# The gap in front of the key stacks taken out of a cross-attention kernel

## The reference

```
x (256 x 512), ctx (25088 x 512)
# 1. cross attention with sigmoid scores, 16 heads of 32
q = layernorm(x) Wq^T / sqrt(32);  k = ctx Wk^T;  v = ctx Wv^T
x = x + (sigmoid(q k^T per head) v) Wo^T
# 2. causal self attention over the 256 rows without softmax, each row divided by exp(n)
# 3. feed-forward: silu(h w1) * (h w2), two gelu layers of 2048, and back to 512
```

## Time and profile before

| | kernel before |
|---|---|
| time, median of 3 | 1910.59 us (1910.14 to 1911.89) |
| profiled execution | 1911.86 us, span of its instructions 1910.1 us |
| TensorE: matmul busy, weight load busy | 1899.6 us, 1709.3 us |
| VectorE busy | 1199.5 us |
| ScalarE busy | 1016.6 us |
| matmuls L749, L774, L790, L810 | 4032, 4032, 3136, 6272 records |
| granted TensorE clock | full speed (2.4 GHz) in all 40 slices of the span |

### The profile page before, as it was taken

How to read it: one execution, slowest core, us unless ns; L and a number is a source line. 1 busy time by engine, 2 the same in 40 slices (tenths; PEclk the granted TensorE clock), 3 DMA queues, 4 the chain that set the end, 5 groups by cost and what they waited for, 6 DMA issues and landing times.

```text
span 1910.1 us, 50764 instructions
## 1 busy us (share of the span) xinstructions
PE 1899.6 (99%) x19347; PEld 1709.3 (89%) x19348; DVE 1199.5 (63%) x2109; ACT 1016.6 (53%) x1136; POOL 4.5 (0%) x17
## 2 busy tenths in 40 slices
PE   9999999999999999999999999999999999999999
PEld 8889999999898999999888999999988999867998
DVE  7576766667667576666766757666676675427322
ACT  5545455555545545555554555545455455544864
POOL 0000000000000000000000000000000000000000
PEclk9999999999999999999999999999999999999999
DMA  7556555555655645555565564555556555464784
GB/s 214 154 153 176 133 154 157 158 155 143 171 145 155 172 130 154 156 159 158 144 170 146 152 169 132 158 152 159 157 151 168 143 148 139 100 233 150 279 299 165
DMA packets 130730, 310.91 MB, mean 163 GB/s; under 512 B 33888, under 2 KB 36960, under 8 KB 112096
## 3 DMA queue, kind: packets, MB, share of 16 engines
q1 hardware_dynamic: 97696, 212.79, 41.9%
q10 hardware_dynamic: 32992, 97.53, 15.8%
HBM read 153.95 MB, written 0.52 MB: 81 GB/s over the span
## 4 chain that ended last, share of the span: by engine, by line
PE 98%; DVE 1%; ACT 0%; DMA 0%; issue 0%; DVEq 0%; ACTq 0%
PE kp L749 25%; PE vp L774 24%; PE sc L790 19%; PE acc L810 18%; PE ps L1572 6%; PE ps L1557 2%; PE py L1585 1%; PE qk_p L1281 1%; PE kp L836 1%; PE vp L853 0%; PE sc L870 0%; DVE w_lo L1208 0%; DVE ln_stats L72 0%; PE kp L1059 0%; PE vp L1050 0%; DMA probs<-wkT_dram 0%
## 5 line engine op out<-in xcount | busy, mean ns | idle before, releaser
L378 ACT ACTIVATE probs<-sc 128x1024 f32<-128x1024 f32 x784 | 769.7, 1025 | 730.4 <-PE sc L790 594.6
L749 PE MATMUL kp<-x_combos,weights_r 128*128 128x256 f32 x4032 | 536.0, 279 | 0.0
L749 PEld LDWEIGHTS kp<-x_combos,weights_r 128*128 128x128 f32 x4032 | 491.4, 188 | 28.7 <-issue 28.4
L774 PE MATMUL vp<-more_weights,x_combos 128*128 128x256 f32 x4032 | 515.6, 277 | 0.0
L774 PEld LDWEIGHTS vp<-more_weights,x_combos 128*128 128x128 f32 x4032 | 485.3, 188 | 0.6 <-issue 0.4
L790 PE MATMUL sc<-rows_r,k_stack_r 96*128 96x256 f32 x3136 | 436.4, 279 | 0.1
L790 PEld LDWEIGHTS sc<-rows_r,k_stack_r 96*128 96x128 f32 x3136 | 396.0, 188 | 2.8 <-issue 1.6
L591 DVE TENSOR_TENSOR parts<-parts,kp 128x512 f32<-128x512 f32 x240 | 164.5, 685 | 327.0 <-PE kp L749 327.0
L810 PE MATMUL acc<-probs,v 128*32 128x256 f32 x6272 | 354.4, 380 | 0.0
L810 PEld LDWEIGHTS acc<-probs,v 128*32 128x32 f32 x6272 | 195.9, 110 | 131.4
L528 DVE TENSOR_TENSOR x_combos<-ctx_raw,x_combos 128x512 fp32r<-128x512 f32 x240 | 166.2, 693 | 8.2
(11 more groups left out here) (164 smaller groups left out, 851.5 us busy)
## 6 DMA issues: line engine op xcount, KB each, us to landing
k_stack_r<-k_rows_hi SPq DMA_DIRECT2D x784, 64.0 KB, 2.3
k_stack_r<-k_rows_lo SPq DMA_DIRECT2D x784, 64.0 KB, 2.4
k_stack_r<-k_stack_r SPq DMA_DIRECT2D x196, 256.0 KB, 3.0
ctx_raw<-ctxT_dram ACTq DMA_DIRECT2D x48, 1024.0 KB, 6.3
weights<-w_all_dram ACTq DMA_DIRECT2D x176, 256.0 KB, 3.6
w_raw<-w_all_dram SPq DMA_DIRECT2D x44, 1024.0 KB, 4.8
weights<-wqk_dram SPq DMA_DIRECT2D x2, 1024.0 KB, 11.7
probs<-wvT_dram SPq DMA_DIRECT2D x2, 512.0 KB, 7.5
```

The source lines that it names most:

```text
L378: nc.scalar.activation(probs[:, place(par, n), :], sc[g % 2][:], ACT.Sigmoid).then_inc(probs_ready, 1)
L749: last = nc.tensor.matmul(k2[:, r, :], wk[i - 1][:, k, a, r * P:(r + 1) * P], xc[:, i - 1, k, b, :], start=i in FRESH and r == 0 and n == ...
L774: last = nc.tensor.matmul(v2[:, r, :], xc[:, i - 1, k, b, r * P:(r + 1) * P], wv_c[i - 1][:, k, a, :], start=i in FRESH and r == 0 and n == 0,
```

## The change

One line goes. The 192 bytes per partition in front of `k_stack` are no longer there, so `k_stack` begins 192 bytes lower, and so does every tensor that is allocated behind it in `cross_attention` (`parts`, `k_rows_hi`, `k_rows_lo`, `v`, `probs`, `ln_stats`, `ln_mv`). Counted as above, `k_stack`, `v` and `probs` move from 320 to 128, the place of `more_weights`. No instruction is added, removed or put elsewhere in the order. What is allocated for the self attention and the feed-forward part begins where it did.

```diff
@@ -132,7 +132,6 @@
         wk, wv_c = [first_w[:, i] for i in range(7)], [more_w[:, i] for i in range(7)]
         raw, tmp = sb("ctx_raw", [P, KE, CH]), sb("x_sum", [P, 2, HS])
 
-        gap("before_k_stack", 48)
         kst, kst_f32 = keep["two_types"](stack, "k_stack", [P, 2, 2, HG, 2, HS])
         parts_r, parts = keep["two_types"](stack, "parts", [P, 4, 2, HS])
         kc, vt = parts[:, 0:3], parts[:, 3]
```

## The result

The changed kernel takes 1947.2 us (median of 5 runs, 1945.3 to 1953.0) against 1910.3 us before (5 runs on the same chip): ratio 1.019, 95% interval 1.0176 to 1.0205. It is slower, as forecast, but by 37 us instead of 12. The direction held and the size did not: 1947 is the rival that I gave 0.30.

What follows compares the result with a forecast made beforehand. TensorE, busy 99%, was taken as the bound, by the distance of matmul starts. Scores gave +12 us, other main terms 0, the prologue -0.3 at most: 1910.6 + 12 = 1922.6, rounded 1923; range 1901 to 1952, the forecast's own 1914 to 1930.

Steps and rivals of the forecast that it cites:

- the rival that I gave 0.30: All key and value groups lose the fast rate, 1.41 us instead of 1.36: +30 us, total 1944 to 1953; chance 0.30.
- the first part: Whole kernel: TensorE busy 99%; time is the number of matmuls by the distance of their starts.
- the place of two operands modulo 512: Matmuls: moving less stationary place modulo 512 bytes sets the rate, 113.3, about 117.7 or 120 ns.
- (b): Scores: operand distance goes from 192 to 384, so they run at 120 ns, 0.96 us a group: +12 us.
- the 191 or 192 that I gave as a sign: Scores' weight loads: would last 191 or 192 ns in the mean instead of 188 if the forecast was right.
- the parity of 64-byte steps: Operand distances: odd multiples of 64 (64, 192) reach the floor; even ones (256, 384) collide and run at 120 ns.
- (c): Keys and values behind the scores: keep their distance of 64 and their places, so unchanged, 0.
- (d): Steps from values or keys to scores: at most 5 us lies there, not winnable with scores at 120 ns: 0.
- (e): `weigh`: `v` and `probs` move together, their distance stays 0: 0 us, bounds 6 us either way.
- (f): Prologue: two kinds of product out of `v` go from distance 256 to 448 and 64: -0.3 us at most.
- (g): DMAs into `k_stack` and engine writes of `probs`, `parts`, `v` go 192 bytes lower: 0, bound a microsecond.
- The rival "nothing moves": Whole kernel: TensorE's two read ports are independent, so place cannot matter: 1910.6 us; chance 0.17, "same" finally 0.14.

Runs made afterwards that it cites:

- f1: Kernel before with the 48-float gap behind the key stacks (ahead of `parts`) instead of ahead of them: 1946.6 us, ratio 1.0186.
- f2: Kernel before with its gap ahead of the key stacks kept and 80 floats added behind them, shifting only `parts`, `v`, `probs`: 1911.6 us, ratio 0.9993.
- f4: Kernel before with 64 unused bytes ahead of `weights`, so all matmul operands move together: 1911.1 us, ratio 0.9992.
- m1: Kernel before with gaps ahead of `x_combos`, `more_weights`, `k_stack` of 96, 16, 16 floats instead of 64, 16, 48: 1924.4 us, ratio 1.0055.
- m3: Kernel before with gaps ahead of `x_combos`, `more_weights`, `k_stack` of 64, 48, 16 floats instead of 64, 16, 48: 1925.9 us, ratio 1.0063.
- D = 64: Kernel before with 80 instead of 48 gap floats ahead of the key stacks; scores' moving less stationary place 64 bytes modulo 512: 1944.4 us, ratio 1.0174.
- f3: Kernel before with key stacks split by chunk half, half 0 at scores' operand distance 384, half 1 behind the gap at 192: 1931.9 us, ratio 1.0102.
- m2: Kernel before with gaps ahead of `x_combos`, `more_weights`, `k_stack` of 96, 16, 32 floats instead of 64, 16, 48: 1926.9 us, ratio 1.0068.
- D = 448: Kernel before with 112 instead of 48 gap floats ahead of the key stacks; scores' moving less stationary place 448 bytes modulo 512: 1912.5 us, ratio 1.0004.
- 128: Kernel before with 64 instead of 48 gap floats ahead of the key stacks; scores' moving less stationary place 128 bytes modulo 512: 1951.9 us, ratio 1.0205.
- k1: Kernel before with gaps ahead of `x_combos`, `more_weights`, `k_stack` of 96, 48, 0 floats instead of 64, 16, 48: 1940.1 us, ratio 1.0140.

## Why the prediction was right and wrong

- *That no transfer and no other engine sets the time, and that only the distance between starts can move* (the first part): right. The counts are the same, PE is at 99% in both, and the growth of the three fp32r lines is 36.5 of 37.0 us. In the whole run the scores' matmuls sat idle for 2.0 us, 1.9 of them the wait in the prologue.
- *That the place of two operands modulo 512 sets that distance*: right in part. f1, f2 and f4 show that of what the change moved only the stacks matter, and that it is their place relative to the other operands. The period is 256, not 512. That the pair is the scores' own two operands, and not the stacks and what the group ahead streams, is not shown, and m1 and m3 say that a group's own distance is not enough.
- *(b), the scores go to 120 ns, +12 us*: near. They start 0.95 us / 8 = 119 ns apart, and their line grew by 8.8 us; their weight loads last 189 ns in the mean, not the 191 or 192 that I gave as a sign. The reason was not borne out: I took 64 and 192 for one class and 256 and 384 for the other by the parity of 64-byte steps. D = 64 at 1944.4 us breaks it as a rule for the time of the kernel.
- *(c), keys and values unchanged, 0*: this step failed, and it is the 25 us by which the forecast missed. It rested on one prologue group that went on at the floor behind a group at distance 256, against the values behind 30.69 in the same rows that did not. I had the right mechanism written down as a rival: the scores were the only place in the loop where the rate was seen to come back. It said 600 groups by 0.05 us, 30 us; keys and values grew by 27.7 (14.1 + 13.6). With 12 or less for the scores it gave 1944 to 1953, and 1947.2 is inside. f3 and m2 show that mechanism. It is not quite all groups: 23 of the 336 value groups still end at the floor. The chances were wrong because I costed the changed group by itself and took its neighbours, whose addresses don't move, as out of reach, though rows 6 and 7 showed one line at two rates with all its own addresses the same. Such a line can only be slow for what ran ahead of it.
- *(d), the steps between groups, 0*: their worth in the changed kernel can't be told from the scores' own rate. D = 448 is no test of it: its steps into the scores are those of 192 modulo 256. As the cause of the loss the steps are a rival that no run here excludes: the first three scores behind the values are at 118 to 120 ns before the change too.
- *(e), `weigh` and the shift of `v` and `probs`, 0*: right, 354.4 us in both profiles and f2 at ratio 0.9993.
- *(f)*: right. The four groups out of `v` took 1.44, 1.44, 1.57 and 1.36 us where they had 1.43, 1.54, 1.61 and 1.44: 0.2 us less together. In the first three, 190 ns or more pass between the first two matmuls; only the last is free of that, and it runs at the floor:

```profile
29.17 1.52 PE L852 MATMUL vp<-v_r,x_combos 128*128 128x256 f32 x12
30.53 1.52 PE L852 MATMUL vp<-more_weights,x_combos 128*128 128x256 f32 x12
```

- *(g), the DMAs*: right for the loop; the wait and the clock in the prologue are not of this change, some 2 us in that execution. Such a wait stands in 7 of the 17 profiled executions (0.8 to 1.9 us), in that of f2 too, whose stacks lie as before (1.25 us); only in this one, the longest, did the granted clock fall behind it.
- *The rival "nothing moves"*, from the Trainium skill, "SBUF — State Buffer", section "Who interferes with whom": "PE and ACT never wait on anyone". By that reading the time would have stayed; it grew by 1.9% for 192 bytes of place, so for the time of this kernel the measurement decides against it. What the runs can't tell is whether it is the memory or the array's own sequencing of two independent reads that is late.

What stays open is the mechanism below the rate: why the step into the scores loses it, and why 192 modulo 256 brings it back behind some groups and not behind others. The trace shows only starts, and no run separates the reads themselves.

## What to carry to other kernels

Where TensorE is the bound, as here with its weight loads 89% busy, look at the distance between the starts of equal matmuls, group by group. If one line with fixed operands has two rates, ask whether the rate is handed on from the group ahead, as it was here; then changing one group's operands is to be costed over all the groups behind it. Try places with gaps in steps of 64 bytes over 256, as in this sweep, and look for a group that brings the fast rate back, not for one that is fast alone. Remove such a gap only with a measurement: it holds nothing, and here it was worth 1.9%.

## What the runs showed that I had not expected

The feed-forward matmuls, all at distance 192, ran through at one of two rates in whole executions. In the profile of s448 (D = 448):

```profile
1774.59 60.47 PE L1572 MATMUL ps<-weights_r,w_hi 128*128 128x256 f32 x512
1834.89 1.81 PE L1572 MATMUL ps<-rows_r,w_hi 128*128 128x256 f32 x14
```

That is 117.8 ns each over 512 matmuls (60.30 us between the starts) where the kernel before had 113.3; over all 1280 such matmuls it is 5.7 us (150.9 against 145.2 from start to start). With one kind of matmul and nothing between that changes the pattern, whichever rate it starts at stays.

The 17 profiled executions of this document know only these two values: 58.03 us for the 512 in eleven, 60.30 in six (D = 64, 128 and 448, k1, m1 and m3). The six took 5.1 to 5.8 us more than the fastest run of the same kernel; the eleven took 0 to 3.5 more, the 3.5 being the changed kernel with its wait in the prologue. So this is the likely reason why single runs of the kernel before, 19 beside f1 to f4, spread from 1909.9 to 1920.9 us. What sets the rate at which the part starts is open.
